# A conditioned graph-attention and transformer block: products for x, condition and k as four column tiles side by side in the set-up, and the q/k/v stage's normalization and head loads in pieces

## The reference

```python
# L0
q_exp = jnp.where(row_zero[..., None], 0.0, q[:, None, :])
self_feat = jnp.concatenate([v, q_exp], -1) @ W_self.T + b_self
for d in range(2):
    kv = self_feat[:, :20]
    qh = (self_feat @ Wq[d].T + bq[d]); kh = (kv @ Wk[d].T + bk[d])
    aff = einsum(qh, kh) / sqrt(32); aff = where(mask, aff, NEG) + label_bias
    output += einsum(softmax(aff), kv) -> Wout[d] + bout[d]
x = v + relu(output)
# L1
shift, scale, gate, ... = split(silu(cond) @ Wt + bt, 6)
h = layernorm(x) * (1 + scale) + shift
q, k, v = h @ Wqkv + bqkv
x = x + gate * (softmax(q k^T / sqrt(32)) v @ Wproj + bproj)
x = x + gate2 * mlp(layernorm(x) * (1 + scale2) + shift2)
```

## Time and profile before

| | |
|---|---|
| median of 3 runs | 3301.62 us (3296.03 to 3301.97) |
| profiled execution | 3298.79 us, its span 3296.7 us |
| TensorE busy | 3167.4 us, 96% |
| VectorE busy | 1948.7 us, 59% |
| ScalarE busy | 1569.3 us, 48% |
| GpSimd busy | 1621.4 us, 49% |
| mean granted TensorE clock | 0.982 |

### The profile page before, as it was taken

The page is one execution under the profiler, slowest core; times in us unless marked ns, Lnnn a source line. Parts: engine busy times, 40 slices in busy tenths (PEclk is TensorE's granted clock), DMA queues, the critical chain, the costliest instruction groups (busy, mean ns, idle before and its releaser), DMA issues. The chain is left out here.

```text
span 3296.7 us, 44393 instructions
## 1 busy us (share of the span) xinstructions
PE 3167.4 (96%) x16788; PEld 2161.6 (66%) x16788; DVE 1948.7 (59%) x3352; ACT 1569.3 (48%) x2887; POOL 1621.4 (49%) x808
## 2 busy tenths in 40 slices
PE   7899989899999999999999999999979799999998
PEld 5688878777555555555555555555437688888887
DVE  2478764465878778778787787787436322222221
ACT  0122224333666666666666666666645432222222
POOL 2366530000878878778788788787763000000000
PEclk9999989999999999999999999999989899999999
DMA  5143324634767766768667677667467421111100
GB/s 197 53 136 99 125 77 175 196 126 147 189 164 172 185 157 149 180 153 202 162 152 175 164 173 184 155 151 180 112 181 272 163 74 42 42 42 41 42 20 13
DMA packets 198866, 446.93 MB, mean 136 GB/s; under 512 B 65871, under 2 KB 87631, under 8 KB 167942
## 3 DMA queue, kind: packets, MB, share of 16 engines
q1 hardware_dynamic: 140006, 250.23, 22.4%
q0 software_dynamic: 18432, 134.23, 20.5%
q10 hardware_dynamic: 40224, 59.78, 7.7%
HBM read 157.39 MB, written 84.44 MB: 73 GB/s over the span
## 5 line engine op out<-in xcount | busy, mean ns | idle before, releaser
L1380 DVE TENSOR_REDUCE heads_mx<-att_pM 128x1 f32<-128x512 f32 x1960 | 1200.9, 680 | 323.7 <-PE att_pM L1428 322.7
L1365 ACT ACTIVATE att_prob<-att_pS 128x512 f32<-128x512 f32 x2048 | 1047.4, 618 | 349.0 <-PE att_pS L1477 340.7
L1298 POOL TENSOR_TENSOR att_acc<-att_acc,att_prob 128x2048 f32<-128x2048 f32 x224 | 1036.0, 4625 | 204.6 <-ACT att_prob L1365 193.2
L1445 PE MATMUL att_pO<-att_prob,att_V 128*32 128x512 f32 x4096 | 497.4, 603 | 0.0
L1477 PE MATMUL att_pS<-heads_q,heads_k 98*128 98x512 f32 x1024 | 424.3, 414 | 5.8 <-POOL att_ks L1257 5.8
L1477 PE MATMUL att_pS<-att_qs,att_ks 98*128 98x512 f32 x1024 | 424.6, 419 | 2.3 <-ACT att_prob L1365 2.1
L1428 PE MATMUL att_pM<-att_ks,att_qs 96*128 96x512 f32 x1024 | 408.3, 399 | 0.0
L2010 PE MATMUL mlp_pu<-mlp_hs,mlp_W 128*128 128x512 f32 x1536 | 370.5, 390 | 12.4 <-POOL mlp_hs L1953 12.4
L1428 PE MATMUL att_pM<-heads_k,heads_q 96*128 96x512 f32 x936 | 374.5, 400 | 0.0
L2010 PEld LDWEIGHTS mlp_pu<-mlp_hs,mlp_W 128*128 128x128 f32 x1536 | 289.4, 188 | 73.0 <-POOL mlp_hs L1953 12.8
L1940 ACT ACTIVATE mlp_tu<-mlp_pu,keep_cols 128x512 f32<-128x512 f32 x128 | 88.3, 690 | 503.8 <-PE mlp_pu L2010 503.8
(11 more groups left out here) (242 smaller groups left out, 3751.2 us busy)
## 6 DMA issues: line engine op xcount, KB each, us to landing
att_gathered<-att_prob POOLq DMA_DIRECT2D x128, 1024.0 KB, 8.1
att_gathered<-att_prob SPq DMA_DIRECT2D x64, 1024.0 KB, 6.5
qk_d<-graph_LW SPq DMA_DIRECT2D x64, 512.0 KB, 2.8
heads_q<-qk_d ACTq DMA_DIRECT2D x21, 512.0 KB
heads_k<-qk_d ACTq DMA_DIRECT2D x21, 512.0 KB
att_qs<-qk_d ACTq DMA_DIRECT2D x21, 512.0 KB, 7.1
att_ks<-qk_d ACTq DMA_DIRECT2D x21, 512.0 KB, 10.5
gat_xT<-in_xT SPq DMA_DIRECT2D x32, 256.0 KB, 3.3
```

Of the source, the lines that this page charges most:

```text
L1298: nc.gpsimd.tensor_tensor(acc[half][:], old[:], new[:], ALU.add).then_inc(added, 1)
L1365: nc.scalar.activation(prob[step % PR][:, c, :], pS[at % 3][:], ACT.Exp, scale=SCALE).then_inc(exp_done, 1)
L1380: nc.vector.tensor_reduce(mx[:, q // 4, q % 4:q % 4 + 1], bank(at)[:], AX.X, ALU.max).then_inc(m_read, 1)
L1445: last = nc.tensor.matmul(pO[c * HD:(c + 1) * HD, :], V[g % 2][:, mt, (c // 2) * HD:(c // 2 + 1) * HD], prob[step % PR][:, c, :], start=mt ...
```

## The change

In the set-up, the condition and x products are turned round: the 32-column pads of the condition and the 20 columns of x are stationary, `WsT` moves (512 columns), and the four results (two batches of condition, two of x) stand in four column tiles of `pb0`. They are copied to `rows_a`, and four transposes turn them to columns. The condition rows stay in `rows_a`, so that the later product in rows falls away; only the two `one3` products are left (in `pb5`). The k product is done the same way (four tiles: two batches, two directions), copied and turned. `Gs` goes through four banks. The small x loads and the product with ones stand ahead of the load of `WsT`; the memsets are put in another order and chained.

In q/k/v, `norm` is cut into four pieces that stand behind the first four entries of `ORDER`, whose first transposes come one tile later; the head loads go out per chunk, six transfers behind the third entry of the chunk that follows. In attention, TensorE's wait for the memset moves into the first `finish`.

```diff
+            pe.wait_ge(ld_x, 32)
+            pe.wait_ge(cleared, 4)
             for c in range(DC):
                 last = mm(pb[2][:, 0:40], ones[:], xT20[:, c].rearrange("p b m -> p (b m)"), c == 0, c == DC - 1)
+            for c in range(DC):
+                for b in range(B):
+                    mm(pb[0][32 * b:32 * b + 32, :], pads[:, COND + c * B + b, :], WsT[:, DC + c, :], c == 0, c == DC - 1)
+                for b in range(B):
+                    last = mm(pb[0][64 + 32 * b:64 + 32 * b + NONGT, :], xT20[:, c, b, :], WsT[:, c, :], c == 0, c == DC - 1)
+            last.then_inc(rows_done, 1)
+            pe.wait_ge(rows_kept, 2)
+            for j in range(DC):
+                last = nc.tensor.transpose(pb[1][:, j * P:(j + 1) * P], rows_a[:, j * P:(j + 1) * P], ident[:])
...
-            for d in range(2):
-                for j in range(DC):
-                    for c in range(DC):
-                        last = mm(pb[3][:, (d * DC + j) * 40:(d * DC + j + 1) * 40], WkT[:, d, c, j * P:(j + 1) * P],
-                                  sf20[:, c, :], c == 0, c == DC - 1)
+            for c in range(DC):
+                for n in range(4):
+                    last = mm(pb[3][32 * n:32 * n + 32, :], sf20[:, c, n // 2, :], WkT[:, n % 2, c, :], c == 0, c == DC - 1)
             last.then_inc(kt_done, 1)
+            pe.wait_ge(kt_kept, 1)
+            for j in range(DC):
+                last = nc.tensor.transpose(pb[4][:, j * P:(j + 1) * P], rows_b[:, j * P:(j + 1) * P], ident[:])
...
+            g_banks = (4, 5, 1, 2)
             for n in range(16):
                 d, fc, half = n // 8, n // 2 % 4, n % 2
-                if n >= 2:
-                    pe.wait_ge(G_ready, n - 1)
+                if n >= 4:
+                    pe.wait_ge(G_ready, n - 3)
...
-        ORDER = [("q", 0), ("q", 1), ("v", 0), ("q", 2), ("h", 0), ("q", 3), ("h", 1), ("v", 1), ("q", 4), ("h", 2), ("q", 5),
-                 ("v", 2), ("h", 3), ("q", 6), ("q", 7), ("v", 3)]
+        ORDER = [("q", 0), ("q", 1), ("v", 0), ("q", 2), ("q", 3), ("h", 0), ("v", 1), ("h", 1), ("q", 4), ("h", 2), ("q", 5),
+                 ("h", 3), ("v", 2), ("q", 6), ("q", 7), ("v", 3)]
...
+            def load_heads(i):
+                at = slice(i * 512, (i + 1) * 512)
+                for x in (q_stored[0], q_stored[1], q_stored[2], q_stored[3]):
+                    sp.wait_ge(x, 16 * 2 * (i + 1))
+                for r in range(3):
+                    sp.dma_start(raw(first_q[r * HD:(r + 1) * HD, :, at]), q_v[(0, 0, 1)[r], :, :, at]).then_inc(heads_loaded, 16)
+                    sp.dma_start(raw(first_k[r * HD:(r + 1) * HD, :, at]), k_v[(0, 1, 0)[r], :, :, at]).then_inc(heads_loaded, 16)
...
+                    if e == 3 and 1 <= i <= HEADS:
+                        load_heads(i - 1)
...
+            def norm_behind(e, i, s):
+                if e == 0:
+                    row_stats(i, s, (0, 1))
+                elif e == 1:
+                    row_stats(i, s, (2, 3))
+                    variances(i)
+                elif e == 2:
+                    factors(i)
+                    normal(i, s, (0, 1))
+                elif e == 3:
+                    normal(i, s, (2, 3))
...
+                if n == 0:
+                    pe.wait_ge(cleared, U)
                 sums(pS[at % 3], prob[(n % 2 * MT + LAST) % PR], True, False)
...
-            pe.wait_ge(cleared, U)
```

More of the change, by code:

```diff
@@ L248, in _ @@
         def _(pool):
-            nc.gpsimd.memset(VB[:], 0.0).then_inc(cleared, 1)
-            nc.gpsimd.memset(Kblk[:], 0.0).then_inc(cleared, 1)
-            nc.gpsimd.memset(raw(r4[:]), 0.0).then_inc(r4_cleared, 1)
[L252 to L258, removed]
+            for i, (tile, value) in enumerate(((ones[:], 1.0), (pads[:], 0.0), (one3[:], 0.0), (one3[:, 0:1], 1.0), (sf20[:], 0.0),
+                                               (rows_a[64:P, :], 0.0), (rows_a[0:64, :], 0.0), (Kblk[:], 0.0), (VB[:], 0.0))):
+                if i:
+                    pool.wait_ge(cleared, i)
+                nc.gpsimd.memset(tile, value).then_inc(cleared, 1)
+            pool.wait_ge(cleared, 9)
+            nc.gpsimd.memset(raw(r4[:]), 0.0).then_inc(r4_cleared, 1)
+            pool.wait_ge(ld_w, 16)
             for b in range(B):
@@ L415, in _ @@
             pe.wait_ge(pads_ready, 3)
-            for c in range(DC):
-                for b in range(B):
-                    q, e = slice(32 * b, 32 * b + 32), slice(64 + 32 * b, 96 + 32 * b)
-                    last = mm(pb[0][q, :], pads[:, COND + c * B + b, :], WsT[:, DC + c, :], c == 0, c == DC - 1)
-                    if c == 0:
-                        mm(pb[0][e, :], one3[:], rows_in[:], True, True)
+            for b in range(B):
+                last = mm(pb[5][64 + 32 * b:96 + 32 * b, :], one3[:], rows_in[:], True, True)
             last.then_inc(row_done, 1)
@@ L906, in body @@
             def body(i, s):
-                if before(i, NCH - 1):
-                    root(i + 1)
-                for kind, j in ORDER:
+                for e, (kind, j) in enumerate(ORDER):
+                    if e == 2 and before(i, NCH - 1):
+                        root(i + 1)
                     if kind == "q":
@@ new lines, in normal @@
+            def normal(i, s, rows):
+                if at_least(i, 1) and rows[0] == 0:
+                    dve.wait_ge(tr_done, i * 4)
+                for nt in rows:
+                    nc.vector.tensor_scalar(xn[:, nt, :], xr[s][:, nt, :], mv[:, nt, 0:1], rstd[:, nt:nt + 1],
+                                            ALU.subtract, ALU.mult).then_inc(xn_ready, 1)
+            def norm_behind(e, i, s):
[9 more added lines that the diff above has]
+                    normal(i, s, (2, 3))
```

149 lines of the change are left out of this document (86 added, 63 removed).

## The result

The changed kernel takes **3275.57 us** (median of 4 runs, 3273.45 to 3282.75) against 3298.82 us for the kernel before on the same chip (4 runs, 3290.63 to 3301.97): ratio 0.9935, 95% interval 0.9922 to 0.9948. It is 23 us faster. The forecast was 3257, with 3244 to 3272: the direction was right, the gain came out little more than half the 42.8 us of the sum.

What follows compares the result with a forecast made beforehand. TensorE, busy nearly the whole span, was taken as the bound. Set-up 19.5, heads 11.5, normalization 8.8 - 2.0, first chunk 0.3 and attention 4.7 summed to 42.8 us: forecast 3257 us, range 3244 to 3272 (8 in 10).

Steps and rivals of the forecast that it cites:

- Rows product: Set-up: sixteen 512-column matmuls on four column tiles, beginning at 14.7 us and taking 6.0 us.
- rival 3: Set-up: 32- and 20-column tiles in turn don't overlap, sixteen matmuls take 13.8 us, 20 us given back: 3277; chance 0.04.
- The gap behind it: Set-up, rows to columns: copy 0.7, transposes 1.1, small operations 1.8, in all 3.6 us; k product begins at 24.3.
- k product, gap, G: Set-up: k product 5.5 us, copy to hand-overs 3.8, G 11.0 instead of 12.9, ending at 44.6, 17.6 earlier.
- Rival 2: Set-up stays at half clock to G's end (6.9, 6.9 and 12.9 us): set-up gains 15, total 3262; chance 0.10.
- the rule that the prediction set against itself: Set-up: transposes don't count as clock activity, so the k product starts cold and costs about 6.5, 1 us more.
- The Wt wait: Set-up: TensorE reaches the second modulation 13.3 us after G's end and waits 2.7 us for Wt.
- the term of +1.9: Set-up behind G: 1.9 us gained on top of the 17.6 us at G's end.
- Heads: q/k/v, chunk 4: quarter loads behind each chunk hide the 8.87 us wait and its clock loss; 11.5 us gained.
- Rival 1: q/k/v: the heads' last quarter is late, TensorE waits 3 us at 640 and loses the clock: 3264; chance 0.10.
- The normalization in pieces: q/k/v: stalls of 11.8 us become 3.0 over two chunks, gaining 8.8; 0.4 lost in each of chunks 0 to 4.
- Attention: Attention's start: the moved memset wait lets TensorE start 3.7 us earlier, plus 1.0 for the clock.

Runs made afterwards that it cites:

- GpSimd late: Changed kernel with GpSimd's two subtractions of LW waiting for the last G copy: 3273.63 us, ratio 0.9920 to the kernel before.
- third maxima elsewhere: Changed kernel, still 43 slots, with the three slots of three maxima moved to the last chunk (v0, q5, v3): 3277.95 us, ratio 0.9933.
- the run from the fifth slot on: Changed kernel with maxima from chunk 4's fifth slot on (44 slots instead of 43) and heads' loads one entry earlier: 3276.38 us, ratio 0.9923.
- the last kernel: Changed kernel with GpSimd's subtractions behind G, condition columns from PSUM, WoutT halved, third maxima behind last-chunk v tiles, projection weights later: 3254.75 us, ratio 0.9865.
- WoutT in halves: Changed kernel with the first half of WoutT's load sent when half of G is done: 3272.88 us, ratio 0.9921.

## Why the prediction was off

**Rows product: right.** 13.48 to about 19.3, 5.8 us (6.0). It began 1.2 us earlier than taken (14.7). Tiles of 32 and 20 columns in turn do overlap; rival 3 is out. **The gap behind it: the first step that failed.** The prediction took 1.8 us for the small operations, "eight become four and three are added", by their count and size. It did not ask where their operands lie and what GpSimd does meanwhile. They took 5.50 us at L301 alone. The whole gap, 3.6 us in the sum, took 8.1, and 3.2 with GpSimd late; k started at 27.39 instead of 24.3, and with GpSimd late at 23.34. In the kernel before the eight read PSUM and ran behind GpSimd's subtractions,

```profile
18.41 9.00 POOL L263 TENSOR_TENSOR graph_LW<-set_WsT,graph_LW 128x2048 fp32r<-128x2048 f32 x2
...
30.34 1.26 DVE L287 TENSOR_SCALAR set_qnz<-set_pb,set_pads 128x20 f32<-128x20 f32 x8 [8.49 <-PE set_pb L367]
```

so its trace showed no such cost; the overlap of the two engines on the new time line could have been read from GpSimd's row.

**k product, gap, G.** 5.64 (5.5), 3.6 (3.8) and 8.93 us (11.0), G at full clock from its first matmul; G's end 45.5 against 44.6. That this is only 0.9 us late is luck: the early start of the rows product and the 2.1 us that G fell short of its 11.0 cover most of what the gap cost. In the eight profiles with this set-up unchanged the k product took 5.3 to 6.6 us and G 8.9 or 10.6 to 11.9: when the clock falls and comes back differs from run to run, and the start of the graph stage with it (114.8 to 118.4). Rival 2, half clock up to G's end, held in none in full; the worst had k at 6.58 and G at 11.91. By the rule that the prediction set against itself, that transposes don't hold the clock, k starts cold; 3.64, 5.09 and 5.12 us behind the same four transposes show that it need not, and leave open what the transposes do.

**The Wt wait: mechanism right, size wrong.** Foreseen 2.7 us, measured 4.62, and 4.2 to 5.0 in the other seven. TensorE got there 13.5 us behind G's end, as forecast (13.3), but Wt came 18.2 us behind it where the sum took 16.0 from the kernel before; why the transfers took 2.2 us more is open. The loss behind it was not in the sum at all: the stop takes the clock and the modulation costs 5.2 to 6.6 us instead of 3.45. So the term of +1.9 became about -3, which is nearly the whole shortfall of the set-up in this profile. I had the rule in my own text (a stop of 3 us cost the clock at 682) and didn't apply it to the wait that I forecast.

**Heads: right.** No wait where 8.87 us stood; from chunk 4's first transposes to chunk 5's, 58.5 us became 42.3, with the normalization's 5 in it (16.5 in the sum). The 11.5 by themselves were not measured. The margin of 1 us was real. Rival 1 did not come, but it does as soon as the maxima start one product earlier (2.35 us).

**The normalization in pieces: right in kind, its place not.** Stalls at the blocks gone, 0.4 us at the transposes, 0.5 lost in each of chunks 0 to 4 (0.4). From chunk 5's first transposes to chunk 6's it took 45.8 us before and 42.1 with the third maxima elsewhere: 3.7 gained, where the sum had 3.8. The step that failed is one I had left out: with the chunk's new order and `e >= 6` for `e >= 5`, chunk 4 has seven slots instead of eight, so that 43 in place of 44 carry the 89 uses of the banks. Three slots then hold three maxima instead of one, and a third behind a q costs 2.2 us of waiting; chunk 5 was 4.3 us shorter without it (46.4 to 42.1, the clock's part in it). Measured against the run from the fifth slot on, which has none before the last slot, two of them cost 8.4 us in the first profile and 6.8 in the second, of the 8.7 and 8.1 missing in q/k/v. The sum of one division in `maxima_behind` would have shown it.

**Attention: the last step that failed.** The first score came at the stage's start, 3.7 us earlier, as forecast. But the prediction took it that these 3.7 us, and 1.0 more for the clock, would last to the end. ScalarE waited 1.5 to 4.7 us for a buffer that a late transfer held, and the first output copy came 2 to 7 us later after the first score. The memset's wait had hidden SyncE's queue: "what is late next" was asked in the set-up and not here.

Set-up 13.0 for 19.5, q/k/v 14.2 for 22.3, attention -5.8 for +1.0: 21.4 for 42.8. Each cause was taken away by itself, and all together brought 42.5. That this meets the forecast's number is in part luck: it is 24.2 for 19.5 in the set-up, 19.6 for 22.3 in q/k/v and 1.3 for 1.0 in attention. The share of each in the totals is less sure than in the profiles, since single edits of 3 to 5 us lie near what medians tell; and why the clock comes back when it does is open.

## What to carry to other kernels

When an operation moves, look at what every engine does at its new time, and where its operands lie: a short VectorE operation with both inputs in SBUF can wait for a long one of GpSimd. When a stop is taken away, name the next thing in the queue that was hidden by it, and price the clock for every stop that you forecast yourself. Where work is dealt to slots by a division, work the division out: one slot fewer made two stalls.

## What the runs showed of the hardware

VectorE with two SBUF inputs beside a GpSimd subtraction: 5.50 us for 0.53 us of work, and 4.98 for 0.68 in both kernels that put the subtraction beside it. GpSimd itself lost nothing (8.97, 9.00 and 9.08 us). With one input in PSUM there was no cost at all. Matmuls on four column tiles with 32 and 20 columns in turn overlapped: sixteen of 512 columns in 5.8 us, part of it at half clock. A stop of TensorE of 2.2 us cost the clock in one profile of the changed kernel (736.75, a product of 4.48 us behind it) and not at the same place in the other:

```profile
737.08 4.48 PE L1099 MATMUL qkv_pq<-graph_LW,graph_W 128*128 128x512 f32 x12
...
733.71 0.50 PE L1070 MATMUL qkv_pM<-heads_k,heads_q 96*128 96x512 f32 x1 [2.21 <-DVE heads_mx L1010]
734.04 2.88 PE L1099 MATMUL qkv_pq<-graph_LW,graph_W 128*128 128x512 f32 x12
```

A stop of 2.24 us ahead of the second modulation cost it in the last kernel (5.33 us), one of 2.05 with WoutT in halves did not (3.63); stops of 4.2 to 5.0 us at that place cost it in all ten profiles that have them.
